# Expert blocks of a mixture-of-experts kernel: W1 and W3 as the stationary operand of the up projection, from a copied place

## The reference

```
def swiglu(x, w1, w2, w3):
    return jax.nn.silu(x @ w1) * (x @ w3) @ w2
B, S, D, H, E = (.., .., 256, 128, 32)
Hs = 2 * H
...
scores = jax.nn.softmax(xf @ Wg, axis=-1)
weights, indices = jax.lax.top_k(scores, TOP_K)          # TOP_K = 4
for e in range(E):
    ...                                                  # the rows xg of expert e, their weights w
    out = swiglu(xg, W1[e], W2[e], W3[e]) * w[:, None]
    y = y.at[tok].add(out)
z = swiglu(xf, Ws1, Ws2, Ws3)                            # shared, hidden size Hs
return (y + z).reshape(B, S, D)
```

## Time and profile before

| | |
|---|---|
| median of 3 runs | 856.4 us (855.65 to 857.94) |
| the profiled execution, own time | 855.39 us |
| its span | 853.6 us |
| mean granted clock of TensorE | 0.968 of full speed |
| PE busy in the span | 772.0 us, 90% |
| ACT busy / DVE busy | 444.5 us, 52% / 505.9 us, 59% |
| first and last silu of the expert stage | 520.3 and 789.1 us |

### The profile page before, as it was taken

The page is one execution under the profiler, slowest core; times in us unless marked ns, Lnnn a source line. Parts: engine busy times, 40 slices in busy tenths (PEclk is TensorE's granted clock), DMA queues, the critical chain, the costliest instruction groups (busy, mean ns, idle before and its releaser), DMA issues.

```text
span 853.6 us, 17128 instructions
## 1 busy us (share of the span) xinstructions
PE 772.0 (90%) x3742; PEld 586.5 (69%) x3743; DVE 505.9 (59%) x1499; ACT 444.5 (52%) x1828; POOL 378.4 (44%) x352
## 2 busy tenths in 40 slices
PE   6866999999999999999967849999999999999995
PEld 4655577777776767667745427887787877788554
DVE  1774236485959587776846544555555555555388
ACT  2445767776776768576713102555455555555110
POOL 1001332324756474747576162555555555555200
PEclk9989999999999999999998789999999999999999
DMA  7345223324443344499478386667676765555797
GB/s 249 99 138 170 87 86 119 112 88 135 162 157 134 134 155 140 165 292 362 161 245 313 111 292 217 191 214 221 193 223 200 229 207 179 166 180 159 278 408 333
DMA packets 104454, 164.38 MB, mean 193 GB/s; under 512 B 10885, under 2 KB 87763, under 8 KB 102867
## 3 DMA queue, kind: packets, MB, share of 16 engines
q1 hardware_dynamic: 90227, 120.02, 43.6%
q0 software_dynamic: 13824, 41.96, 13.4%
q10 hardware_dynamic: 352, 1.80, 0.6%
HBM read 90.01 MB, written 78.97 MB: 198 GB/s over the span
## 4 chain that ended last, share of the span: by engine, by line
PE 60%; DVE 10%; issue 9%; DMA 8%; ACT 5%; POOL 3%; SPq 2%; ACTq 2%; another core or an unknown queue 1%; DVEq 0%; POOLq 0%
PE psum L1639 13%; PE psum L1487 12%; PE psum L1522 11%; PE psum L1394 10%; PE psum L1653 6%; PE psum L1562 3%; DVE big L1357 3%; DMA big<-in_x 2%; ACT sm L828 2%; DMA xblk<-expert_lists 2%; POOL expert_lists L672 2%; PE psum L1577 2%; PE psum L1417 1%; DVE st L954 1%
## 5 line engine op out<-in xcount | busy, mean ns | idle before, releaser
L710 POOL DMA_INDIRECT y_d<-sm,yrow x160 | 155.4, 971 | 132.7 <-issue 91.3
L1639 PE MATMUL psum<-big,xbT 128*128 x640 | 166.5, 383 | 3.7 <-DVE xbT L1327 3.1
L672 POOL DMA_INDIRECT expert_lists<-rows,slot x128 | 127.1, 993 | 86.6 <-DVE slot L1171 47.9
L828 ACT ACTIVATE sm<-psum,nmax 128x77 f32<-128x77 f32 x512 | 157.6, 369 | 5.7 <-DVE nmax L1188 2.5
L1487 PE MATMUL psum<-big,xnT 128*128 (+2 forms) x384 | 143.0, 522 | 9.2 <-ACT sm L828 8.6
L1522 PE MATMUL psum<-big,pT 128*128 (+1 forms) x640 | 143.6, 379 | 0.0
L1522 PEld LDWEIGHTS psum<-big,pT 128*128 128x128 f32 x640 | 119.1, 190 | 14.9
L828 ACT ACTIVATION_READ_ACCUMULATOR sm<-psum,nmax 128x1 f32 x512 | 128.3, 251 | 0.0
L688 POOL TENSOR_TENSOR sm<-sm,sinv 128x1232 f32<-128x1232 f32 x32 | 72.0, 2249 | 125.6 <-DVE sinv L1225 125.4
L1639 PEld LDWEIGHTS psum<-big,xbT 128*128 128x128 f32 x640 | 109.1, 190 | 15.9 <-issue 7.4
L1487 PEld LDWEIGHTS psum<-big,xnT 128*128 128x128 f32 x384 | 71.2, 193 | 69.0 <-issue 52.8
(11 more groups left out here) (190 smaller groups left out, 1004.4 us busy)
## 6 DMA issues: line engine op xcount, KB each, us to landing
xblk<-expert_lists SPq DMA_DIRECT2D x160, 160.0 KB
y_d<-zero SPq DMA_DIRECT2D x32, 512.0 KB
big<-y_d SPq DMA_DIRECT2D x8, 2048.0 KB, 16.5
big<-in_L_ffn_W SPq DMA_DIRECT2D x16, 320.0 KB
xin<-in_x SPq DMA_DIRECT2D x36, 128.0 KB
big<-in_x SPq DMA_DIRECT2D x8, 512.0 KB, 3.5
xres<-in_x SPq DMA_DIRECT2D x8, 512.0 KB, 4.9
x_d<-x SPq DMA_DIRECT2D x8, 512.0 KB, 3.0
```

What stands on the lines that cost most here:

```text
L672: pool.indirect_dma_start(out=lists, out_offset=bass.IndirectOffsetOnAxis(ap=slot[:, ph, tt, k:k + 1], axis=0), in_=rows[:, ph, tt, :], in ...
L710: pool.indirect_dma_start(out=y_d, out_offset=bass.IndirectOffsetOnAxis(ap=yrow[:, q:q + 1], axis=0), in_=eo[:, q, :], in_offset=None).the ...
L828: last = nc.scalar.activation(sm[:, t % 2, h * SK:(h + 1) * SK], head_scores(h, h + 1), ACT.Exp, bias=nmax[:, t % 2, h:h + 1], accum_out=s ...
L1639: last = mm(bank(2 + q % 2)[:, 0:2 * H], xbT[:, q % 2, k, :], ew[:, bass.ds(e, 1), k * 2 * H:(k + 1) * 2 * H], start=k == 0, stop=k == KC - 1)
```

## The change

`block_up` swaps its operands. W1 and W3 are now stationary, in four matmuls of 128 moving columns (`xbT`) instead of two of 256, and the result has the hidden features on the partitions, the 128 rows along the free axis. That is the form in which `block_down` takes its stationary operand, so `block_hT`, the copy to `ehT` and their semaphores are gone, and `block_down` uses `eh` itself, at a lag of 3 instead of 4. The weights are not taken from `ew`, whose address depends on the expert, but from `w_now`, a place with two buffers: ACT copies the block's W1 there (`copy_w1`), DVE its W3 (in `move_block`, behind the copy of `xbT`). DVE now reads the table of experts too. ACT's copy for block b stands in its slot b behind silu(b-1), and waits for `eh_psum` of block b-2, whose weights had the same buffer.

```diff
-    AT_UP, AT_HT, LAG = 1, 3, 4
+    AT_UP, LAG = 1, 3
...
+        w_now = sb("w_now", [P, 2, 2, KC, H])
...
+            def copy_w1(b, q, e):
+                wait(act, "eh_psum", b - 1)
+                nc.scalar.activation(w_now[:, q % 2, 0, :, :], ew[:, bass.ds(e, 1), 0:2 * D]
+                                     .rearrange("p o (k i h) -> p (o k) i h", k=KC, i=2)[:, :, 0, :], ACT.Copy).then_inc(s["w1_ready"], 1)
+
             def silu(b, q, _):
                 wait(act, "eh_ready", b - 1)
                 wait(act, "eh_psum", b + 1)
-                nc.scalar.activation(eg[:, q % 2, :], bank(2 + q % 2)[:, 0:H], ACT.Silu).then_inc(s["eg_ready"], 1)
+                nc.scalar.activation(eg[:, q % 2, :], bank(2 + q % 2)[:, 0:P], ACT.Silu).then_inc(s["eg_ready"], 1)
...
-            turns(act, {AT_UP: silu, LAG: move_eo}, (AT_UP, LAG), ACT_TURN, packed_table(act, "column", 2, ACT_TURN))
+            turns(act, {0: copy_w1, AT_UP: silu, LAG: move_eo}, (AT_UP, 0, LAG), ACT_TURN,
+                  packed_table(act, "column", 2, ACT_TURN))
...
-            def move_xbT(b, q, _):
+            def move_block(b, q, e):
                 wait(dve, "eh_psum", b - 1)
                 wait(dve, "xbT_psum", b + 1)
                 nc.vector.tensor_copy(xbT[:, q % 2, :, :].rearrange("p k n -> p (k n)"), bank(q % 2)[:, 0:D]
                                       ).then_inc(s["xbT_sbuf"], 1)
+                nc.vector.tensor_copy(w_now[:, q % 2, 1, :, :],
+                                      ew[:, bass.ds(e, 1), 0:2 * D].rearrange("p o (k i h) -> p (o k) i h", k=KC, i=2)[:, :, 1, :]
+                                      ).then_inc(s["w3_ready"], 1)
 
             def gate(b, q, _):
-                wait(dve, "ehT_psum", b + (1 - NH4))
+                wait(dve, "eo_psum", b + (1 - NH4))
                 wait(dve, "eg_ready", b + 1)
-                nc.vector.tensor_tensor(eh[:, q % NH4, :], eg[:, q % 2, :], bank(2 + q % 2)[:, H:2 * H], ALU.mult
+                nc.vector.tensor_tensor(eh[:, q % NH4, :], eg[:, q % 2, :], bank(2 + q % 2)[:, P:2 * P], ALU.mult
                                         ).then_inc(s["eh_ready"], 1)
 
-            def move_ehT(b, q, _):
-                wait(dve, "eo_psum", b - 1)
-                wait(dve, "ehT_psum", b + 1)
-                nc.vector.tensor_copy(ehT[:, q % 2, :], bank(4 + q % 2)[:, 0:P]).then_inc(s["ehT_sbuf"], 1)
-
-            turns(dve, {0: move_xbT, AT_UP: gate, AT_HT: move_ehT}, (0, AT_HT, AT_UP), NX)
+            turns(dve, {0: move_block, AT_UP: gate}, (0, AT_UP), NX, packed_table(dve, "of_w3", 2, NX))
...
-            def block_up(b, q, e):
+            def block_up(b, q, _):
                 wait(pe, "eh_ready", b - 1)
                 wait(pe, "xbT_sbuf", b + 1)
-                for k in range(KC):
-                    last = mm(bank(2 + q % 2)[:, 0:2 * H], xbT[:, q % 2, k, :],
-                              ew[:, bass.ds(e, 1), k * 2 * H:(k + 1) * 2 * H], start=k == 0, stop=k == KC - 1)
+                for i in range(2):
+                    wait(pe, "w3_ready" if i else "w1_ready", b + 1)
+                    for k in range(KC):
+                        last = mm(bank(2 + q % 2)[:, i * P:(i + 1) * P], w_now[:, q % 2, i, k, :], xbT[:, q % 2, k, :],
+                                  start=k == 0, stop=k == KC - 1)
                 last.then_inc(s["eh_psum"], 1)
-
-            def block_hT(b, q, _):
-                if isinstance(b, int) and b < 2:
-                    wait(pe, "z_added", 2 * MID)
-                wait(pe, "ehT_sbuf", b - 1)
-                wait(pe, "eh_ready", b + 1)
-                transpose(bank(4 + q % 2)[:, 0:P], eh[:, q % NH4, :]).then_inc(s["ehT_psum"], 1)
 
             def block_down(b, q, e):
                 wait(pe, "eo_ready", b - 1)
-                wait(pe, "ehT_sbuf", b + 1)
-                mm(bank(6 + q % 2)[:, 0:D], ehT[:, q % 2, :], ew[:, bass.ds(e, 1), 2 * D:3 * D], start=True, stop=True
+                wait(pe, "eh_ready", b + 1)
+                mm(bank(6 + q % 2)[:, 0:D], eh[:, q % NH4, :], ew[:, bass.ds(e, 1), 2 * D:3 * D], start=True, stop=True
                    ).then_inc(s["eo_psum"], 1)
 
-            turns(pe, {0: block_T, AT_UP: block_up, AT_HT: block_hT, LAG: block_down}, (0, AT_UP, AT_HT, LAG), PE_TURN,
+            turns(pe, {0: block_T, AT_UP: block_up, LAG: block_down}, (0, AT_UP, LAG), PE_TURN,
                   packed_table(pe, "expert", 1, PE_TURN))
```

More of the change, by code:

```diff
@@ L220, in attention_moe_kernel @@
         xbT = sb("xbT", [P, 2, KC, P])
-        eg = sb("eg", [P, 2, H])
-        eh = sb("eh", [P, NH4, H])
-        ehT = sb("ehT", [P, 2, P])
+        eg = sb("eg", [P, 2, P])
+        eh = sb("eh", [P, NH4, P])
+        w_now = sb("w_now", [P, 2, 2, KC, H])
         eo = sm[:, :, :].rearrange("p i n -> p (i n)")[:, 0:NX * D].rearrange("p (q d) -> p q d", q=NX)
@@ L265, in attention_moe_kernel @@
             s_psum s_silu s_gated z_psum z_added
-            xbT_psum xbT_sbuf eh_psum eg_ready eh_ready ehT_psum ehT_sbuf yrow_ready eo_psum eo_ready
+            xbT_psum xbT_sbuf eh_psum eg_ready eh_ready w1_ready w3_ready yrow_ready eo_psum eo_ready
             ysum_step""".split()}
@@ L1321, in _ @@
             phase1_over(dve)
-            def move_xbT(b, q, _):
+            dve.wait_ge(s["tab_ready"], 2)
+            def move_block(b, q, e):
                 wait(dve, "eh_psum", b - 1)
```

## The result

The changed kernel took 919.6 us (median of 4 runs, 913.4 to 921.7) beside 856.8 for the kernel before: a ratio of 1.071, 95% interval 1.067 to 1.075, 62.8 us slower. The forecast was 918, with a range of 886 to 950. The profiled execution took 918.4 us, 63.0 more than that of before.

A forecast was written before the change was run, and what follows sets the result against it. A ring through ACT's silu and W1 copy and PE's up was taken to bound: 1.96 us plus 0.10 for table loads, times 159, plus 4 of stalls, 331.5 against 268.8, drain 1 less: 918 us, range 886 to 950.

The forecast's parts named there:

- end of up to silu, first load and up: Between PE and ACT: 0.20 us from up's end to silu, 0.10 for the unhidden first load, 0.88 for up.
- silu to copy: On ACT: 0.24 us from silu's start to the next instruction, W1's copy, with three register instructions between.
- copy to load: From ACT's copy to PE's weight load: 0.12 us for the release, bounds 0.05 and 0.23.
- ring: Expert stage, from one up's end to the next through ACT's silu and W1 copy: 1.96 us a block.
- block with the table load: Every fourth block, ACT's table register load stands between silu and copy: 0.38 us more, about 2.34 between silus.
- stalls kept: Expert stage: 4 of the 9.6 us of scattered stalls stay, since rows arrive in time more often.
- DVE's copy is free: DVE's W3 copy, bounds nothing and 0.42 us, is hidden by PE's slot, being needed over 1 us later.
- The small pairs cost nothing: PE's up as 8 pairs of load and 128-column matmul, 0.11 us apart: 0.88 us against 0.87 before.
- rival of a shorter ring: ACT's register work runs ahead of silu: 1.9 us a block or less, 875 to 890 us; 5 in 100.
- hidden copy: ACT's copy is hidden and PE bounds at 1.53 us a block: 16 us less, 840 us; chance 0.04.
- granted clock: Rival: PE's clock falls to 1.2 GHz in the expert stage, 3.06 us a block, 1078 us; 3 in 100.
- the copy was not slow: Rival: ACT's SBUF copy as slow as line 773's, 2.33 us a block, 961 us; 6 in 100.

The follow-up runs named there:

- e3: The changed kernel with ACT's register load of the expert table issued a slot earlier for 30 of 40 loads: 904.6 us, ratio 1.055.
- e5: The changed kernel with ACT copying W1 twice behind silu, first to a spare place nobody reads: 967.8 us, ratio 1.129.
- e6: The changed kernel with ACT's copy of W1 ahead of silu and doubled, one copy to a place nobody reads: 888.8 us, ratio 1.035.
- e1: The changed kernel with ACT's copy of W1 for block b moved ahead of silu(b-1): 891.9 us, ratio 1.038.
- e13: The kernel before, with up as 4 matmuls of 128 columns in place of 2 of 256, xbT still stationary: 828.1 us, ratio 1.0016.
- e15: e1's kernel run a second time, on a chip where the kernel before took 823.7 us: 805.8 us, ratio 0.978.
- e2: The changed kernel with up multiplying by W3 first and W1 second, ACT's order kept: 901.7 us, ratio 1.052.
- e4: The changed kernel with W1's copy also on DVE, none on ACT: 887.4 us, ratio 1.032.
- e10: e1 with ACT copying expert 0's W1 for every block, so the copy needs no table register: 895.1 us, ratio 1.042.
- e12: e1 with up as 2 matmuls of 256 columns in place of 4 of 128, second halves of W1 and W3 unused: 802.4 us, ratio 0.971.
- e14: e12's kernel run a second time, on a chip where the kernel before took 823.7 us: 802.5 us, ratio 0.974.

## Why the prediction was right, step by step

| step | predicted | measured |
|---|---|---|
| end of up to silu, first load and up | 0.20 + 0.10 + 0.88 = 1.18 | 1.20 (load 745.52 to silu 746.72) |
| silu to copy | 0.24 | 0.23 |
| copy | 0.42 | 0.416 |
| copy to load | 0.12 | 0.11 (745.41 to 745.52) |
| ring | 1.96 | 1.96, 107 times |
| block with the table load | 2.34 | 2.32 to 2.43, 37 times (0.46 of it the load, by e3) |
| stalls kept | 4 us | 4.2 (three long steps, 10.36 less 3 x 2.06) |
| expert stage | 331.5 us | 332.2 |
| drain | -1 | -1.1 |

- *PE no longer bounds, ACT's copy closes a ring.* Shown by the chain, and by e5 against e6: a second copy costs 48 us behind silu and nothing ahead of it. The first copy moved ahead of silu (e1) takes the undisturbed step from 1.96 to 1.55.
- *DVE's copy is free.* So it was in this order: W3's copy takes 0.28 us, not the bound of 0.42, and no row has anything wait for it.
- *The table load costs 0.38 us in every fourth block.* Nearly: against the plain step of 1.96 it is 0.39, and against the same slot without a load 0.46 (e3). 30 moved loads of 0.38 would be 11.4 us; it took 13 to 15 less.
- *The small pairs cost nothing.* Within 0.03 us a block (e13), with the whole block at 1.55 us in e15.
- *4 us of stalls.* The number came out at 4.2 and the reason did not. I kept 4 by choice, thinking of late rows of `xblk`. 3.6 of the 4.2 are the two long steps at blocks 119 and 120, and they come from one silu that starts 2.5 us after its up, 0.02 us behind PE's signal. Before has such a silu at block 121 (a step of 4.90). That is luck.
- *One sum doesn't come out.* The rival of a shorter ring drops 0.24 and 0.10 us and puts silu's 0.28 in their place: 2.06 - 0.24 - 0.10 + 0.28 = 2.00 us, about 908, and not 1.9 and 875 to 890. Nothing else was built on it, and the ring came out at its full length.
- *The hidden copy as a rival* needed the copy ahead of silu, and the prediction put it at 840 against 856, 16 us less than before. e15 has that order and took 17.9 us less. On the chips of the first eight runs the same order took 34 us more, and for that the prediction had no term: my sum of 1.53 us would have been wrong there by 0.38 a block.
- *What was lucky:* the ring's 0.4 us of waiting per block. In the changed kernel there is no late silu but the one at block 119, although before took 857 us beside it, and in e1's first run, beside a before of 858, there were dozens. That the waiting is what keeps them away is not shown. A forecast for e1 from the same rows missed by 50 us.
- The granted clock stayed, and the copy was not slow; those rivals fell.

## What to carry to other kernels

Order on an in-order engine is a dependence: ahead of a wait a helper's copy was free here, behind it the copy joined PE and ACT into a ring of 1.96 us where PE alone needs 1.53, 0.43 us of new idle PE time a block. Look for the instruction that waits and ask what stands behind it, before counting any engine's slack. And when several different cures stop at the same wrong number, run the best one on another chip before naming a second bound in the code.

## What the runs showed that I had not expected

- Chips differ by about 4% on the same program: 857 us for before on some and 824 to 827 on others. On the first kind there are stalls of some 2 us, in the attention of every kernel (1.8 to 1.9) and in the expert stage of e1, e2, e4, e6 and e10 (mostly 1.7 to 2.2), though hardly in that of before, where PE has as little rest. The sign of a change can hang on it: copy first is 1.038 (1.031 to 1.045) on one and 0.978 (0.976 to 0.981) on another.
- What makes these stalls is open. In e1, e4, e6 and e10 it is PE's signals that come late, four within 0.3 us where the work between them takes 1.53 (33 of 34 times in e1, 34 of 35 in e10, 25 of 28 in e4, 28 of 30 in e6), so PE's records aren't ahead of its work there. In e2 the signal is late too, but the next up's follows only 1.45 us later (median). It isn't ACT's addresses (e10), ACT's copy (e4) or its length (e6).
- One rival fits the counts of the expert stage and was not tested: how many instructions PE's stream needs per us, loads, matmuls and register instructions together. From the 11th to the 151st silu, e15 has 20.0 a us. On the first kind of chip no traced kernel is above 16.3: e1 and e6 16.2, e10 16.1, e4 16.0, e2 15.7, and before, with one late silu, 16.2 as well. If that were the limit of the first kind, e1's 31.5 instructions would take 1.94 us a block, which is its mean there (1.95), and e12 (23.3 a block, 15.1 a us) would have no late silus on such a chip, while e13 (37.7 a block) would have many. Against it stands the attention, whose holes come at 10.7 to 10.9 a us. Neither kernel was run on such a chip: e12, e13 and e14 all ran on chips without the stalls. The changed kernel was not run on a chip without them either, so what the change costs there is not known.
- The 128x256 copy from SBUF on ACT took 416 ns, 33 more than the 383 from PSUM, while two in a row start 0.32 us apart.
